# Two attention stages of a transformer layer pair: which engine makes the low half of the weights, and where GpSimd's norms stand

## What is computed

```python
xn = _layernorm(x) * ln_gamma + ln_beta            # tokens 2048, width 128
q, k, v = split(xn @ w_qkv)                        # 16 heads of 64
qr, kr = rotate(q), rotate(k)                      # t1*cos - t2*sin, t2*cos + t1*sin
probs = softmax(einsum('bhid,bhjd->bhij', qr, kr) * HD ** -0.5)
out = einsum('bhij,bhjd->bhid', probs, v)          # then @ w_out + b_out, plus a feed-forward part
```

## Time and profile before

| | us |
|---|---|
| median of 3 runs | 3486.61 (3481.0 to 3489.35) |
| the profiled execution's own time | 3484.36 |
| its span, first to last instruction | 3482.6 |
| of it: projection stage 1 (from the page's slices and the rows) | about 1866 to 2040 |
| second attention, 16 heads | about 2044 to 3308 |

### The profile page before, as it was taken

The page is one execution under the profiler, slowest core; times in us unless marked ns, Lnnn a source line. Parts: engine busy times, 40 slices in busy tenths (PEclk is TensorE's granted clock), DMA queues, the critical chain, the costliest instruction groups (busy, mean ns, idle before and its releaser), DMA issues. The chain is left out here.

```text
span 3482.6 us, 59948 instructions
## 1 busy us (share of the span) xinstructions
PE 3037.7 (87%) x19523; PEld 1275.8 (37%) x19523; DVE 2877.3 (83%) x4324; ACT 2989.6 (86%) x2783; POOL 2537.8 (73%) x1581
## 2 busy tenths in 40 slices
PE   6888888888888888888887968999898889989899
PEld 4222112221222212222223424555555555555547
DVE  7989999999999999999997968878887777888421
ACT  3999999999999999999996846878888888878942
POOL 5888888888888888888875524767777776767850
PEclk9788777887778777887778979999999999999999
DMA  2000000000000000000001550100000110000000
GB/s 75 6 8 7 7 0 7 7 7 7 0 7 7 7 7 0 7 7 7 3 6 40 198 143 19 32 26 26 25 26 26 44 32 26 26 26 25 20 22 13
DMA packets 59522, 85.32 MB, mean 24 GB/s; under 512 B 10065, under 2 KB 45905, under 8 KB 58961
## 3 DMA queue, kind: packets, MB, share of 16 engines
q1 hardware_dynamic: 59344, 82.93, 8.3%
HBM read 52.31 MB, written 30.54 MB: 24 GB/s over the span
## 5 line engine op out<-in xcount | busy, mean ns | idle before, releaser
L1264 POOL TENSOR_TENSOR lo<-pr,hi 128x1024 f16<-128x1024 f32 x384 | 883.1, 2323 | 396.3 <-ACT hi L1438 391.1
L1325 DVE TENSOR_REDUCE mx<-mx_ps 128x1 f32<-128x512 f32 x1024 | 660.6, 683 | 127.7 <-PE mx_ps L1480 123.9
L1453 ACT ACTIVATE pr<-s_ps 128x1024 f32<-128x1024 f32 x512 | 533.2, 1041 | 243.4 <-PE s_ps L1511 189.2
L1438 ACT ACTIVATE hi<-pr 128x1024 f16<-128x1024 f32 x512 | 549.3, 1074 | 0.0
L1480 PE MATMUL mx_ps<-ka,qa 128*128 128x512 f16 x1024 | 376.6, 397 | 128.4 <-DVE mx L1325 98.7
L722 ACT ACTIVATE wt<-wt 128x2048 f32<-128x2048 f32 x256 | 485.2, 1896 | 0.5
L713 ACT ACTIVATE wt<-wt,theta_bias 128x2048 f32<-128x2048 f32 (+2 forms) x160 | 482.4, 3015 | 3.2 <-DVE wt L563 2.7
L501 POOL TENSOR_TENSOR wt<-base,wt 128x1024 f32<-128x1024 f32 x192 | 455.3, 2371 | 16.0
L501 POOL TENSOR_TENSOR wt<-vb,wt 128x1024 f32<-128x1024 f32 x192 | 455.1, 2370 | 16.0
L1530 PE MATMUL pv_ps<-vh,hi 128*128 128x129 f16 x4096 | 434.5, 223 | 10.2 <-ACT sums L1444 3.9
L1530 PE MATMUL pv_ps<-vh,lo 128*128 128x65 f16 x4096 | 420.2, 195 | 0.0
(11 more groups left out here) (210 smaller groups left out, 5046.0 us busy)
## 6 DMA issues: line engine op xcount, KB each, us to landing
qk<-stg SPq DMA_DIRECT2D x6, 2048.0 KB, 10.6
vh<-v SPq DMA_DIRECT2D x16, 520.0 KB, 3.4
qa<-qk SPq DMA_DIRECT2D x16, 512.0 KB, 3.6
ka<-qk SPq DMA_DIRECT2D x32, 256.0 KB, 4.8
v<-v_st SPq DMA_DIRECT2D x3, 2080.0 KB, 7.9
qst<-parts_dram SPq DMA_DIRECT2D x144, 32.0 KB
kst<-parts_dram SPq DMA_DIRECT2D x144, 32.0 KB
qk<-stg SPq DMA_DIRECT2D x4, 1024.0 KB, 8.5
```

Source lines behind the costliest of these rows:

```text
L1264: eng.tensor_tensor(lo[:, i % NHL, :, :], pr_slot(i), hi[:, i % NHL, :, :], ALU.subtract).then_inc(lo_done, 1)
L1325: eng.tensor_reduce(mx4[:, q // NCH, q % NCH:q % NCH + 1], mx_ps[:, q % 2, :], AX.X, ALU.max)\
L1438: eng.activation(hi[:, i % NHL, :, :], pr_slot(i), ACT.Copy).then_inc(hi_done, 1)
L1453: eng.activation(pr_slot(i), s_ps[:, i % 2, :, :], ACT.Exp, scale=SM).then_inc(exp_done, 1)
```

## The change

In `stage_attention1`, `on_vector(i)` becomes `i % 32 >= 24`: GpSimd makes the low parts of steps 0 to 23 of each head in a row, VectorE those of steps 24 to 31. The counts in `wait_low` and the start values of the two semaphores follow. VectorE's two halves swap order within a step (second half of the older step first), so that with consecutive steps each half still goes at its time. The number of low parts of each engine stays 24 and 8 a head. In `stage_project1`, GpSimd's 16 norms move from ahead of its low parts to one behind the second low part of each group of four.

```diff
-                for k in range(NT):
-                    eng.tensor_scalar(xn[:, k, :], base[:, k, :], mv[:, k, 0:1], tmp[:, 0, k:k + 1],
-                                      ALU.subtract, ALU.mult).then_inc(xn_ready, 1)
                 for u in range(4 * NT):
...
                                       dst[:, :, 0, :], ALU.subtract).then_inc(lo_ready, 1)
+                    if b == 1:
+                        eng.tensor_scalar(xn[:, k, :], base[:, k, :], mv[:, k, 0:1], tmp[:, 0, k:k + 1],
+                                          ALU.subtract, ALU.mult).then_inc(xn_ready, 1)
...
-    LV = 4
+    NLV = 8
+    NLG = STEPS - NLV
...
         def on_vector(i):
-            return i % LV == LV - 1
+            return i % STEPS >= NLG
...
-                        for n_ in range(2):
+                        for n_ in (1, 0):
                             at = i - LOW - n_
                             if (at >= 0 or not first) and on_vector(at):
                                 low_half(h, at, n_)
...
-                        for n_ in range(2):
-                            low_half(h, STEPS - 1, n_)
+                        low_half(h, STEPS - LOW - 1, 1)
+                        for i in range(STEPS - LOW, STEPS):
+                            for n_ in range(2):
+                                low_half(h, i, n_)
```

More of the change, by code:

```diff
@@ L1249, in on_vector @@
         def on_vector(i):
-            return i % LV == LV - 1
+            return i % STEPS >= NLG
         def wait_low(eng, h, i):
+            before = h + 1 + i // STEPS
             if on_vector(i):
-                eng.wait_ge(lo_vector, STEPS // LV * (h + 1) + i // LV + 1)
+                eng.wait_ge(lo_vector, NLV * before + i % STEPS - NLG + 1)
             else:
-                eng.wait_ge(lo_gpsimd, STEPS // LV * (LV - 1) * (h + 1) + i // LV * (LV - 1) + i % LV + 1)
+                eng.wait_ge(lo_gpsimd, NLG * before + i % STEPS + 1)
         def low(eng, h, i, lo_done):
@@ L1570, in _ @@
                 eng.sem_inc(pv_done, 2 * STEPS)
-                eng.sem_inc(lo_vector, STEPS // LV)
-                eng.sem_inc(lo_gpsimd, STEPS - STEPS // LV)
+                eng.sem_inc(lo_vector, NLV)
+                eng.sem_inc(lo_gpsimd, NLG)
                 eng.sem_inc(s_done, 2 * STEPS)
```

## The result

| | before | after |
|---|---|---|
| median us (runs) | 3483.8 (4; 3481.0 to 3489.4) | 3606.6 (4; 3598.0 to 3609.4) |
| profiled execution: own time / span | 3484.4 / 3482.6 | 3605.2 / 3603.4 |
| heads 1 to 14, mean us of one | 76.5 | 86.1 |
| first head / last head (to the start of its last multiplication), us | 107.9 / 71.3 | 99.3 / 71.3 |

The change makes the kernel slower: ratio 1.0346, 95% interval 1.0323 to 1.037. The forecast was 3596 us, the range 3465 to 3640.

What follows compares the result with a forecast made beforehand. TensorE sets the pace in heads 1 to 14, waiting for VectorE's reductions. Added 15.8 less removed 7.4 us is +8.4 a head, +118 for 14; with -5, +1.5, -2.4 on 3484.4 this gives 3596 us, range 3465 to 3640.

Steps and rivals of the forecast that it cites:

- The takes: Steps 4, 12, 20: GpSimd holds VectorE's addition, then its multiplication; TensorE waits 3.7, 2.9, 3.8 us, 10.4 us a head.
- Rival 1: The take's multiplication passes while GpSimd waits; waits of 2.0, 1.2 and 2.1 us, about 3482 us; chance 0.14.
- rival 2: The takes find GpSimd at rest, costing 0.35 us of TensorE each; 3389 us; chance 0.10 with its mixtures.
- rival 3: GpSimd becomes the bound, its low parts held, a head about 76.5 us; 3480 us, no change; chance 0.06.
- The clock: TensorE's granted clock falls behind the three new waits: 1.8 us each, 5.4 us a head.
- I cost this at nothing: End of a head: VectorE's eight low parts in a row, 16 halves at 0.68 us, hide behind its own rest.
- What is removed: Heads 1 to 14: 4.6 us of waits, 2.3 of clock, some 0.5 of short gaps go: 7.4 us a head.
- The step-3 wait: One TensorE wait stays, behind the second half of step 31 held by GpSimd: 1.1 us in the mean.
- Small parts: Outside heads 1 to 14: first head -5 us, last head +1.5, projection stage -2.4.

Runs made afterwards that it cites:

- e5: Changed kernel with the multiplication of VectorE's take left out, the addition writing straight into the attention's result: 3436.2 us, 0.9851 of the kernel before.
- e6: Changed kernel with the take's addition and multiplication moved from VectorE to GpSimd's own row: 3349.1 us, 0.9604 of the kernel before.
- e9: Changed kernel with each GpSimd low part made by two instructions of 512 columns instead of one of 1024: 3502.1 us, 1.0033 of the kernel before.
- e3: Changed kernel with VectorE's loop over pairs of heads in the second attention written out: 3571.5 us, 1.0245 of the kernel before.
- e8: Kernel before, its old division of low parts kept, with only the take's addition and multiplication moved to GpSimd: 3402.0 us, 0.9747 of the kernel before.
- e1: Kernel before with only the projection stage's part of the change, the moved GpSimd norms: 3483.1 us, 0.9987 of the kernel before.

## Why the prediction was right

- **The takes.** Right in place and size: addition held about 2.1 us, multiplication held again behind a waiting GpSimd, three waits of 3.66, 2.89 and 3.77 us a head. e5 and e6 show that these two instructions are the cause. Rival 1 (0.42 us for the multiplication) and rival 2 (takes find GpSimd at rest) fall by the rows of the take, rival 3 by GpSimd's 534 us of idling. By the rule of the Trainium skill (SBUF — State Buffer, "Who interferes with whom") that whoever issues first has the shared ports for its whole length, the multiplication is held; the measured 2.12 us agree. The 6.44 us of e9, several GpSimd instructions long, do not; there the measurement decides.
- **The clock.** At a granted 0.92 over 1206 us the loss is 0.08 x 1206 / 14 = 6.9 us a head, where the forecast had 5.4; part of this is the loop's edge (in e3, without it, the stretch is at 0.93: 5.9 us).
- **A missed term: the loop's edge.** "I cost this at nothing" is the term that failed. The prediction weighed the eight low parts in a row at the end of a head against ScalarE, and not against VectorE's own standstill at the end of a loop pass, which its old idle time had covered. It is worth 35 us by e3.
- **What is removed.** 7.4 us a head was the gain put on the new division. Without the edge the changed kernel's heads last 83.6 us (e3), the forecast's own sum is 76.5 - 7.4 + 15.8 = 84.9; so the balance was 1.3 us a head too high, 18 us, which hides part of the missed term. Waits and stretch of e3's heads 1 to 14 say which term was off:

```profile
PE mx_ps L1484 <- DVE mx L1327: 162.9, 56, 3.8
```
```profile
2153.70:3324.10 1170.40, 993.55 (x9870) 615.78 (x9870) 925.51 (x1317) 892.16 (x953) 729.51 (x336) 0.93 0.10 26
```

  A head of e3 has 11.6 us of waits (forecast 1.1 left and 10.4 added) and 0.07 x 1170.4 / 14 = 5.9 us of clock (forecast 5.4), and 66.1 us besides; a head before had 5.7, 2.3 and 68.5. So 2.4 us went besides waits and clock, where the forecast had estimated 0.5 for gaps too short to be listed (the clock, given to two digits, leaves some 0.4 us open). e8 shows that the old waits had two causes at once, a take that makes VectorE late and a half that then meets GpSimd: with the takes off VectorE about half of them are left (38.1 of 79.5 us), with the new division as well 15.8 (e6). So the 7.4 us are no measure of the division alone (2.7 us).
- **The step-3 wait.** 1.1 us in the mean was taken over from before; it is 1.55 us in head 5 and 0.9 to 1.8 us in the nine heads off the edge, 1.5 in the mean; at the edge, in head 4, two waits make 4.69.
- **Small parts.** First head -8.6 us (forecast -5, within its ends); last head 0.0 (forecast +1.5, within its ends); projection -2.9 us in its stage (forecast -2.4), and too little for e1's times to tell.

The errors partly cancel, so that it is in part luck how near the sum came: on profiled executions heads 1 to 14 came out at +135 us (forecast +118), all the rest at -14 (forecast -6; the projection stage began 2.0 us earlier), the whole at +120.8 against +112.

## What to carry to other kernels

When work on GpSimd is rearranged, look for every VectorE instruction with two SBUF inputs that will be issued while it runs, and count the one behind it too: a free 0.4 us became 2.1, twice, and TensorE's next product 3.7 us late. If such an instruction is short and its result not urgent, put it into GpSimd's own row, where it cost 0.6 us here and turned 3.5% slower into 4% faster. Before idle time on an engine is filled, ask what else it hid: here the end of a loop pass.

## What the runs showed of the hardware

- A jump back in VectorE's loop cost 3.9 to 4.1 us of standing all five times in the changed kernel, each time with a packet of the instruction queue in it, and none in e6, whose passes are shorter by 16 instructions and have no packet of that queue in heads 4 to 13.
- With short GpSimd instructions in an unbroken row, a VectorE addition was kept out far longer than one of them. In the last head of e9, VectorE's addition and GpSimd's row (some 14 of its halves still to come):

```profile
3299.50 16.38 DVE L1364 TENSOR_TENSOR sums<-sums 128x256 f32<-128x256 f32 x1
...
3261.28 54.32 POOL L1267 TENSOR_TENSOR lo<-pr,hi 128x512 f16<-128x512 f32 x48 [15.69 <-ACT hi L1444]
```

The row ends at 3315.60, the addition at 3315.88. Yet two earlier takes met the same row and got in within 0.82 and 1.44 us, and in the changed kernel, with instructions of 1024 columns, no addition was held over 2.13 us. It is not the short instructions alone: in the last head of e6 a half of VectorE's was kept out 5.63 us, through three GpSimd instructions of 1024 columns, until their row ended at 3159.6 us:

```profile
3154.49 5.63 DVE L1370 TENSOR_TENSOR lo<-pr,hi 128x512 f16<-128x512 f32 x1 [10.95 <-ACT hi L1463]
```

What decides whether VectorE gets in between two GpSimd instructions stays open.
